# Causal attention: scores of even and odd heads on the lower and upper 64 rows, maxima in pairs, three shared PSUM banks

## The reference, cut to what matters

```
h = layernorm(x)                                   # 256 wide
q = rope(h @ q_w): 16 heads of 16;  k = rope(h @ k_w), v = h @ v_w: 4 heads of 16
sc = q k^T / sqrt(16), masked above the diagonal   # 2048 x 2048 per head, two batches
x = x + (softmax(sc) @ v) @ o_w
```

## Time and profile before

| | us |
|---|---|
| median of 3 runs (lowest to highest) | 4031.24 (4022.35 to 4035.92) |
| the profiled execution | 4019.58 |
| its span, first to last instruction | 4017.7 |
| PE busy in the span | 3371.3 (84%) |
| DVE busy in the span | 2484.0 (62%) |

### The profile page before, as it was taken

How to read it: one execution, slowest core, us unless ns; L and a number is a source line. 1 busy time by engine, 2 the same in 40 slices (tenths; PEclk the granted TensorE clock), 3 DMA queues, 4 the chain that set the end, 5 groups by cost and what they waited for, 6 DMA issues and landing times. The chain is left out here.

```text
span 4017.7 us, 46219 instructions
## 1 busy us (share of the span) xinstructions
PE 3371.3 (84%) x16242; PEld 1650.9 (41%) x16242; DVE 2484.0 (62%) x5354; ACT 1680.3 (42%) x2670; POOL 1168.8 (29%) x1015
## 2 busy tenths in 40 slices
PE   6899989897668988999988979994997478878799
PEld 2344334342323323333323235552555255555466
DVE  2999999999727768767768613335662244556212
ACT  4556556554213555554555622211121344434332
POOL 2767776667432000221000000000222333311110
PEclk9999999999968999999999989996998688888899
DMA  2222222212141122022121010003122256453100
GB/s 76 74 66 71 70 67 69 67 65 73 48 71 39 25 30 36 26 49 46 21 30 24 10 50 11 11 6 101 62 91 95 80 135 133 119 118 68 35 21 21
DMA packets 187783, 232.16 MB, mean 58 GB/s; under 512 B 56763, under 2 KB 134031, under 8 KB 184195
## 3 DMA queue, kind: packets, MB, share of 16 engines
q1 hardware_dynamic: 184482, 220.84, 21.7%
q0 software_dynamic: 3072, 8.39, 0.7%
HBM read 183.26 MB, written 45.89 MB: 57 GB/s over the span
## 5 line engine op out<-in xcount | busy, mean ns | idle before, releaser
L1287 ACT ACTIVATE g_pT<-PS 128x1024 f32<-128x1024 f32 (+3 forms) x640 | 552.4, 894 | 466.9 <-PE PS L1593 276.7
L379 POOL TENSOR_TENSOR WB<-m_dtx,WB 128x1024 f32<-128x1024 f32 x256 | 600.9, 2351 | 294.3 <-DVE WB L523 262.9
L1433 DVE TENSOR_REDUCE g_mxp<-PS 128x1 f32<-128x512 f32 x768 | 491.8, 686 | 91.4 <-PE PS L1574 87.4
L411 ACT ACTIVATE PS<-m_dt,m_A 128x512 f32<-128x512 f32 x512 | 353.2, 691 | 433.0 <-DVE WB L514 432.4
L1574 PE MATMUL PS<-g_KT,WB 96*128 96x512 bf16 (+3 forms) x1280 | 423.3, 363 | 120.0 <-DVE g_mxp L1433 57.2
L608 PE MATMUL PS<-WB,ident 128*128 128x512 f32 x1024 | 503.0, 614 | 0.0
L514 DVE TENSOR_TENSOR_SCAN WB<-PS,m_state,WB 128x512 f32<-128x512 f32 x384 | 472.2, 1275 | 14.9 <-ACT PS L411 14.7
L1593 PE MATMUL PS<-WB,g_KT 99*128 99x512 bf16 (+3 forms) x1280 | 359.1, 353 | 1.2 <-ACT g_pT L1287 0.6
L1574 PEld LDWEIGHTS PS<-g_KT,WB 96*128 96x128 bf16 x1280 | 110.4, 98 | 503.8 <-DVE g_mxp L1433 260.4
L523 DVE TENSOR_TENSOR WB<-WB,PS 128x1024 f32<-128x1024 f32 x256 | 308.8, 1206 | 5.8 <-PE PS L594 2.4
L1426 DVE CUSTOM_DVE_ANT_0 PS<-PS,g_mq 128x384 f32<-128x384 f32 (+3 forms) x512 | 246.5, 507 | 98.6 <-PE PS L1574 92.0
(11 more groups left out here) (311 smaller groups left out, 5227.8 us busy)
## 6 DMA issues: line engine op xcount, KB each, us to landing
WB<-b_rows SPq DMA_DIRECT2D x256, 256.0 KB, 3.1
WB<-in_L_ffn_w SPq DMA_DIRECT2D x18, 1024.0 KB, 7.5
WB<-g_dq SPq DMA_DIRECT2D x96, 128.0 KB, 4.1
g_rden<-g_dn SPq DMA_DIRECT2D x128, 64.0 KB, 2.0
w_dv<-WA SPq DMA_DIRECT2D x16, 512.0 KB, 4.5
w_V<-w_dv SPq DMA_DIRECT2D x16, 512.0 KB, 10.7
w_rden<-w_dn SPq DMA_DIRECT2D x128, 64.0 KB, 2.1
g_dq<-g_parts SPq DMA_DIRECT2D x16, 384.0 KB, 2.5
```

Source lines behind the costliest of these rows:

```text
L379: pool.tensor_tensor(hh[:, g % RING, :, :], dtx[:, MB * h:MB * h + MB, :], Bs[:, g % BRING, :].unsqueeze(1) .broadcast_to([P, MB, CH]), AL ...
L411: act.activation(PS[:, 2 + b, :], dt[:, c % 2, m, :], ACT.Exp, scale=Aneg[:, n, m:m + 1]).then_inc(dA_ready, 1)
L1287: act.activation(pT[:, n % 2, 2 * pair:2 * pair + 2, 0:width], PS[:, 2 * pair:2 * pair + 2, at:at + width], ACT.Exp, scale=DH ** -0.5).the ...
L1433: dve.tensor_reduce(mxp[:, q % 6, i % QB, hh:hh + per, at], scores[:, :, 0:width], AX.X, ALU.max)\
```

## The change

The causal attention gets its own plan (`CausalPlan`) and its own stage; the band attention keeps the old ones.

- **Rows.** Even heads keep their 96 rows of parts and the maxima at rows 96 to 98. Odd heads have their parts at rows 64 to 127 and 0 to 31, and the maxima at 32 to 34; rows 35 to 63 are zero. `KT` is kept twice, once for each placement. A maximum now reads only the four pairs of parts in rows 0 to 63 (even) or 64 to 127 (odd); the turned scores read 99 or 128 rows and all six pairs.
- **Maxima in pairs.** One "max" is two matmuls of 64 rows, one on each half of the array's rows, into two banks, and two DVE reduces. On the diagonal two matmuls of 128 columns add the mask on PE (`identb` with `mask_q`), and DVE only reduces.
- **Banks.** 4, 5 and 7 are one ring of three for the maxima and all other uses; each use waits for the bank's last reader.
- **Order.** The pairs are placed at whole windows: pair (heads 2, 3), T0, pair (heads 0, 1), T1, product. Where two groups of maxima are due in one window, the second follows the product. By the new list 39 pairs stand ahead of window 0 (78 maxima, 76 before) and 601 behind it: 372 full ones off the diagonal, 229 on it; 255 windows hold two pairs, 19 hold four, 30 none. The old list has 76 maxima ahead of window 0, then 234 windows with four, 52 with five and 29 with none.
- **Loads.** A build is 25 DMAs, `QT` has a ring of three, `KT` and V six regions. Builds stand 6 windows ahead. The reciprocal stands 4.5 windows behind a block's close, the multiply 9, the outputs 10.5 (before: 3, 6 and 7).
- **Opening.** POOL also clears rows 32 to 63 of `KT` and of the odd heads in `QT` (6144 bf16 elements per row each). SP waits for that, issues 12 DMAs of ones, and only then loads `o_w`.

```
+MAX_BANKS = (4, 5, 7)
+QSLOTS, KREGIONS = 3, 6
+HALVES = ((0, 16, 32, 48, 64, 80), (64, 80, 96, 112, 0, 16))
+MAIN = (slice(0, 64), slice(64, P))
+SHIFT = (96, 32)
+USED = (99, P)
+SPLIT = ((0, 0), (0, 1), (1, 0), (1, 1), (2, 0), (0, 2))
...
+        lead, build_lead, step, rate = 5.5, 6, 0.6, 1.06
+        told, multiplied, projected, gap = 4.5, 9, 10.5, 0.7
...
+        for m, ((q, w), n) in enumerate(zip(maxima, when)):
+            early, late = (0.6, 0.65) if m and when[m - 1] == n else (-0.01, 0.24)
+            acts += [(n + early, "max", 2 * m, q, 2, w), (n + late, "max", 2 * m + 1, q, 0, w)]
...
+        def wait_build(eng, u):
...
+            if u >= QSLOTS:
+                eng.wait_ge(pv, first[2 * (u - QSLOTS) + 2])
+            if u >= KREGIONS:
+                eng.wait_ge(pv, first[2 * NJ * ((u - KREGIONS) // NJ + 1)])
...  SP
+                sp.wait_ge(blank, 2)
+                for e in range(2):
+                    for u in range(KREGIONS):
+                        sp.dma_start(KT[SHIFT[e]:SHIFT[e] + 3, u, :, e, :],
...
+                sp.wait_ge(zeroed, 1)
...
+                        for e in range(2):
+                            for row, (qp, kp) in zip(HALVES[e], SPLIT):
+                                rows = slice(row, row + DH)
+                                sp.dma_start(QT[rows, u % QSLOTS, e:NHP:2, :],
...
+                                sp.dma_start(KT[rows, region(s, c), :, e, :],
...  POOL
+                pool.memset(KT[32:64, :, :, 1, :], 0.0).then_inc(blank, 1)
+                pool.memset(QT[32:64, :, 1:NHP:2, :], 0.0).then_inc(blank, 1)
...  DVE
+                        for e in range(2):
+                            r = ring["max", m] + e
+                            dve.wait_ge(mx, 2 * m + e + 1)
+                            scores = bank(r)[:, 0:width]
+                            to = mxp[:, q % 6, i % QB, hh + e, k0 // CH:k0 // CH + 1]
+                            ins = dve.tensor_reduce(to, scores, AX.X, ALU.max)
+                            ins.then_inc(bank_free[r % 3], 1)
...  PE
+                def claim(i):
+                    if i >= 3:
+                        pe.wait_ge(bank_free[i % 3], i // 3)
...
+                        for e in range(2):
+                            claim(ring["max", m] + e)
+                        for e in range(2):
+                            mm = pe.matmul(bank(ring["max", m] + e)[:, 0:width],
+                                           QT[MAIN[e], u % QSLOTS, 4 * g + hh + e,
+                                              P * (i % QB):P * (i % QB) + P],
+                                           KT[MAIN[e], region(s, k0 // CH), g, e, 0:width],
+                                           start=True, stop=not m_width)
+                            if not m_width:
+                                mm.then_inc(mx, 1)
+                        if m_width:
+                            for e in range(2):
+                                pe.matmul(bank(ring["max", m] + e)[:, m0:m0 + m_width],
+                                          k.identb[:, :], mask_q[:, :], start=False, stop=True)\
+                                    .then_inc(mx, 1)
```

More of the change, by code:

```diff
@@ L9 @@
+import math
 from contextlib import ExitStack
@@ L1660, in _, with __init__ @@
                         mm.then_inc(w_full, 1)
-def stage_causal_attention(k):
-    stage_attention(k, True)
+MAX_BANKS = (4, 5, 7)
[5 more added lines that the diff above has]
+SPLIT = ((0, 0), (0, 1), (1, 0), (1, 1), (2, 0), (0, 2))
+class CausalPlan:
+    def __init__(self):
+        scores, turned = causal_windows()
+        lead, build_lead, step, rate = 5.5, 6, 0.6, 1.06
+        told, multiplied, projected, gap = 4.5, 9, 10.5, 0.7
+        span, apart = 12, (6, 18)
+        self.windows, self.first = [], []
+        for q in range(NQ):
+            self.first.append(len(self.windows))
+            self.windows += [(q, w) for w in turned[block_of(q)[1]]]
+        self.first.append(len(self.windows))
+        acts = []
+        for n in range(len(self.windows)):
+            acts += [(n, "turn", n, 0), (n + 0.25, "turn", n, 1), (n + 1.45, "pv", n)]
+        maxima = [(q, w) for q in range(NQ) for w in scores[block_of(q)[1]]]
+        at, when, ended, began = float("inf"), [], {}, {}
+        for q, w in reversed(maxima):
+            at = min(at, self.first[q] - lead)
+            ended.setdefault(q, at)
+            at -= 1 / rate
+            began[q] = math.floor(at) - 0.02
+            when.append(math.floor(at))
+        when.reverse()
+        self.last_max = {}
+        for m, ((q, w), n) in enumerate(zip(maxima, when)):
+            early, late = (0.6, 0.65) if m and when[m - 1] == n else (-0.01, 0.24)
+            acts += [(n + early, "max", 2 * m, q, 2, w), (n + late, "max", 2 * m + 1, q, 0, w)]
+            self.last_max[q] = 2 * m + 1
+        uses = []
+        for q in range(NQ):
+            closed = self.first[q + 1] + 0.45
+            uses.append((ended[q] + 1.0 + step, "rows", q))
+            uses += [(closed + projected + 1.2 * gap * r, "out", q, r) for r in range(2)]
+            acts += [(ended[q] + 0.1, "parts", q), (closed + 0.2, "den", q),
+                     (closed + told / 2, "den_in", q), (closed + told, "inv", q),
+                     (closed + told + 0.1, "inv_out", q),
+                     (closed + (told + multiplied) / 2 - 0.2, "inv_in", q),
+                     (closed + multiplied, "mul", q)]
+        need = []
+        for u in range(NS * NJ):
+            need.append(began[2 * u])
+            acts.append((need[u] - build_lead, "build", u))
+        end = float("inf")
+        prepared = []
+        for b in reversed(range(B)):
+            for c in reversed(range(NJ)):
+                end = min(need[2 * NJ * b + c] - build_lead - 6 * step - 1, end - apart[b])
+                prepared.append((b, c, end - span))
+        for b, c, begin in reversed(prepared):
+            for i, kind in enumerate(("t0", "t1", "q0", "r0", "q1", "r1", "k", "v")):
+                uses.append((begin + i * span / 8, kind, b, c))
+        taken, placed = [], []
+        for kind, way in (("rows", 1), ("out", 1), (None, -1)):
+            chosen = [x for x in uses if x[1] == kind or kind is None and
+                      x[1] not in ("rows", "out")]
+            limit = None
+            for p, *key in sorted(chosen, key=lambda x: way * x[0]):
+                p = p if limit is None else way * max(way * p, way * limit)
+                for y in sorted(taken, key=lambda y: way * y):
+                    if abs(y - p) < gap - 1e-9:
+                        p = y + way * gap
+                limit = p
+                taken.append(p)
+                placed.append((p, *key))
+        self.use, self.item, self.source, ready = {}, {}, [], {}
+        for i, (at, *key) in enumerate(sorted(placed)):
+            self.use[tuple(key)] = i
+            acts.append((at, "use", *key))
+            kind = key[0]
+            if kind == "out" and key[2] and key[1] % 2 and block_of(key[1])[0] % 2:
+                acts.append((at + 1.0, "stats", key[1]))
+            if kind == "rows":
+                acts.append((at + 2 * step, "rows_in", *key[1:]))
+            if kind == "t0":
+                acts.append((at - 4 * step, "hn", *key[1:]))
+            if kind in ("r0", "r1", "k"):
+                it = len(self.item)
+                self.item[("q" + kind[1] if kind[0] == "r" else kind, *key[1:])] = it
+                self.source.append(tuple(key))
+                acts += [(at + step * (j + 1), name, it) for j, name in enumerate(
+                    ("sum", "part0", "rest", "part1", "part2"))]
+                acts.append((at + step * 6, "store", it, *key))
+                ready[key[1], key[2]] = at + step * 6
+            if kind == "v":
+                acts.append((at + 2 * step, "store_v", *key[1:]))
+        for u, p in enumerate(need):
+            assert ready[u // (2 * NJ), u % NJ] < p - build_lead
+        self.order = [a[1:] for a in sorted(acts, key=lambda a: a[0])]
+        self.ring, i = {}, 0
+        for what, *x in self.order:
+            if what == "max":
+                self.ring["max", x[0]] = i
+                i += 2
+            elif what == "use":
+                self.ring[tuple(x)] = i
+                i += 1
```

504 lines of the change are left out of this document (added).

## The result

| | before | changed |
|---|---|---|
| median of 16 runs each, us | 4025.31 | 4051.54 |
| lowest to highest | 4014.59 to 4036.52 | 4040.68 to 4062.71 |
| profiled span | 4017.7 | 4045.0 |
| start of the causal stage | 1091.28 | 1093.36 |
| product of window 0 | 1240.13 | 1242.92 |

The ratio is 1.0066, 95% interval 1.0055 to 1.0077: slower by 0.66%, some 26 us, on the side and within the range of the forecast. From the start of the stage to window 0 it took 149.6 us (148.9 before), from window 0 to window 319 1119.4 (1088.2 before). The loop of the windows lost 31.2 us where I had put nothing in sum, and the opening lost 0.7 where I had put 10. Behind the loop the spans differ by 7 us the other way; that part varies by as much from profile to profile in the experiments (1679.6 to 1693.8 us).

What follows compares the result with a forecast made beforehand. The prediction took the ring through PE and DVE, neither engine alone, as the bound; its terms summed to +10 us on the profiled 4019.6, giving 4030 profiled and 4041 for the median, range 3985 to 4105.

Steps and rivals of the forecast that it cites:

- D: Whole kernel: the change does what it says but ring and order cancel; the forecast itself, 4019 to 4062; chance 0.45.
- Step 1: Plain windows (two pairs of full maxima): 3.01 us instead of 3.16, gain 0.15 in each of 186 windows, -28 us.
- rival A: Pairs of maxima: they do not overlap (4096) or each switch costs a full drain (4075), so slower; chance 0.20.
- Step 2: Diagonal windows: masks and switches on PE add +0.18 us in the mean, 229 / 2 windows, +21 us.
- Step 3: Outputs: in a ring of three banks none waits for another, 64 x -0.13 = -8 us.
- the ring: Plain window, product to product: the chain through PE and DVE sets its time, 3.16 us before, 3.01 forecast.
- Step 4: Shared ring of banks: 29 small transposes of the maxima delay the pair behind, +8 us (0 to +18).
- Step 5: Doubled windows: 19 with eight maxima, 48 us, against 34 for the old list's extra maxima; remainder +7 us.
- Step 6: Builds: three old DVE stalls go, -25 us; PE waits for builds 6, 10 and 14 instead, +25 us.
- The rival that the loads decide: Builds: one holds PE 10 us or more, or old stalls remain, +25 to +35 us, slower; chance 0.10.
- Step 7: Opening: +6 us to the first maximum, and +4 us for the maxima ahead of window 0.
- Rival B: Causal stage: PE is the bound after all, so faster, 3996 down to 3953; chance 0.25.

Runs made afterwards that it cites:

- e8_pair_late: Changed kernel with only the second pair of maxima moved behind the second turned pair; 0.9851 of the kernel before, loop 1033.2 us.
- the best version: Changed kernel with the second pair behind T1 and each build's 25 transfers issued in two parts; 0.9809 of the kernel before, loop 1013.1 us.

## Why the prediction was right, and where it was not

The sign held, and 4051.54 lies in the range of 3985 to 4105 and in that of D, 4015 to 4065. The mechanism held in outline: ring and order eat up what the pairs save. The size did not (+26 us measured, +10 forecast), and the sign owes something to luck. The sum had nothing for the loop and its +10 for the opening; it was the loop that lost 31.2, and the opening 0.7. By its steps:

*Step 1, plain windows, -28.* Two of its three unknowns held. The second matmul of a pair costs nothing beside the first. A change of shape costs 0.09: 0.31 from a pair's start to the next weights, a slot of 0.22 and 0.09; without the overlap 0.53, twice 0.22 and 0.09. The Trainium skill (TensorEngine Tiling (Array Packing), Key Properties) says that changing the tiling mode drains the engine. The full price of 0.17 does not show in these rows, so that part of rival A falls with the serial pairs. The third, the handover of the bank, was mis-sized: from the end of the first reduce (1563.94 + 0.63) to the pair's start (1564.78) 0.21, not 0.11. Whether the 0.1 more lies in the bank or in the change of shape that comes with it, no run separates. Window 3.12 instead of 3.01, gain 0.04, and 186 x 0.04 = -7 instead of -28. That is the steady window. In the mean the 63 plain windows take 3.16 and the 56 like them before took 3.33, because some of those lay behind an output's window (3.58) or, at the lower level, behind the stall of window 67 (4.58); by that the gain is 0.17, and the step's -28 comes out after all, by another way than mine.

*Step 2, diagonal windows, +21.* I had 0.26 for the mask and its switches in a window; 0.24 to 0.28 was measured by leaving it out, 27 to 30 us in all. The 128 wide window came out at 2.68 (forecast 2.57) and before at 2.33, +0.35 instead of +0.24, again 0.1 where the pair takes its bank. At 512 columns it is 3.40 (forecast 3.27). With 3.16 before, the mean of the two is +0.30, and 229 / 2 windows make +34.

*Step 3, outputs, -8: the step that failed, in its sign.* I costed PE's 0.97 and put DVE's 0.69 into its slack. But the addition stands in DVE's order ahead of the next pair's first reduce, and that reduce is in the ring. An output costs 1.34 in the full window without masks (4.46 less 3.12), 1.18 in the diagonal one of 512 columns (4.58 less 3.40) and 0.96 where there are no maxima (2.93 less 1.97), which is about PE's own time. Against like windows without one, 51 outputs of the changed kernel cost 1.27 in the mean and 37 of the kernel before 1.06, so the 62 of the loop lost some 13 us where I had a gain of 8. A ring of three doesn't help when the third bank's reader stands in the same queue. Moving the outputs gave back 13 to 17 us in the loop.

*Step 4, rows, +8.* Full windows with such a transpose take 3.48 in the mean against 3.12: 29 x 0.36 = +10.

*Step 5, +7,* was not tested alone.

*Step 6, builds.* Both halves came where forecast: no wait of DVE at windows 67, 147, 227 (3.40 each), and new ones of PE at exactly 83, 163 and 243. The waits were half as long as the forecast 5.4 (2.46, 3.21 and 1.48). The price put on them was 25; taking them away gave back 16 to 20, in the order of e8_pair_late. What I had not seen is that a second wait lay under this one: "4.5 windows of slack, just enough" was true only because PE stood still. The rival that the loads decide was wrong in size, but right that they matter.

*Step 7, opening, +6 and +4.* The first maximum came 77.7 us behind the stage's start instead of 81.1, -3.3. The `o_w` loads came 11 us later, `cs` 8.3 later, both from the stage's start. But from `cs` to the store ahead of build 0 it took 19.9 instead of 35.3: the third bank was worth up to 15.4 there, not 12.5 (no run tests it; `cs` also came later, which may have let PE get ahead), and the longer build cost 3.7 (from the store to the first maximum 14.55, before 10.81) instead of 6. From there to window 0 it was +4.0, as forecast.

*Taken together*, the steps as read make -7 + 34 + 13 + 10 + 7 - 25 + 20 = +52 for a loop that lost 31; with the mean plain window in place of the steady one (186 x -0.17 = -32) they make +27. So they are estimates from single kinds of window and no closed account. Of the signs named ahead, two more failed: DVE was idle 0.59 in the plain window and not 0.4 to 0.5, and the first maximum came at 1171.12, ahead of 1175 to 1182.

*Rival B* (PE is the bound, up to -88) was rightly put second for this order: PE was not the bound. With the second pair behind T1 it is, in a plain window, and then the change pays: 1.5% under the kernel before, while the same order without the overlap stays 0.9% above it. The prediction took the written order as given and never asked what the pair's wait could be filled with, though its own sum held 0.44 for T1 right behind that wait.

Open: whether the kernel before would gain by a like change of its order. It was not tried, so how much of the best version's 1.9% is the pairs' doing is not known.

## What to carry to other kernels

Write the ring of a steady window as a sum, and for each wait in it look for the next instruction behind it that does not depend on it: swapping the two was worth 2.2% here, more than all that the change had brought or cost. A small read on a second engine (the output's addition) is in the ring if it stands in that engine's order ahead of the read that frees a bank, however idle the engine is on average. Transfers issued in one block on an in-order queue should be cut where their first reader ends, with the urgent ones of others let in between; issuing the urgent ones first, without the gap, only moved the wait.

## What was not expected of the hardware

- A change between tiles of 64 rows and of 99 or 128 rows costs 0.09 us at each side (0.31 to the next weights behind a pair whose slot is 0.22; 0.97 from T0 to the pair behind T1, four slots and 0.09), the same whether or not the pair overlaps.
- A bank freed by a reduce is taken up by a pair 0.21 behind the reduce's end, where one matmul took 0.12 to 0.16 before.
- Transfers of ones, 12 in 3.80 us, go out every 0.32; those of a build every 0.47.
- POOL clears 32 rows of 6144 bf16 elements in 5.21 us, 0.85 ns an element, near the 0.88 of the earlier trace rows.
